# Product-key weights in chunks of 16 by 8 keys, with both log products of a step in row halves of TensorE

## What is computed

```python
q = (x @ Wq_pk).reshape(b, n, P, HEADS, DIM_KEY)              # P = 2, HEADS = 8
sim = einsum('pbnhd,pkhd->pbnhk', q, pk_keys)                 # two sets of 64 keys
scores, idx = top_k(sim, 16)
score = scores[0][..., :, None] + scores[1][..., None, :]     # sums of pairs of keys
final_scores, final_indices = top_k(score, 16)
w = softmax(final_scores)
k = einsum('bnhk,bnhkd->bnhd', w, keys_table[final_indices])  # 4096 rows a head, 64 wide
v = einsum('bnhk,bnhkd->bnhd', w, values_table[final_indices])
out = causal_attention(q2, k, v) @ Wo                         # q2 = x @ Wq
```

## Time and profile before

| | |
|---|---|
| median of 3 runs | 1949.09 us (1947.84 to 1950.35) |
| profiled execution | 1947.92 us |
| its span | 1946.1 us, granted clock 0.99 |
| TensorE busy | 1868.8 us, 96% |
| weight loads | 1400.6 us, 72% |
| DVE busy | 1608.5 us, 83% |
| ACT busy | 1453.3 us, 75% |
| POOL busy | 1317.2 us, 68% |
| DMA engines | 11.5% on SP's queue |

### The profile page before, as it was taken

The page is one execution under the profiler, slowest core; times in us unless marked ns, Lnnn a source line. Parts: engine busy times, 40 slices in busy tenths (PEclk is TensorE's granted clock), DMA queues, the critical chain, the costliest instruction groups (busy, mean ns, idle before and its releaser), DMA issues.

```text
span 1946.1 us, 43717 instructions
## 1 busy us (share of the span) xinstructions
PE 1868.8 (96%) x11464; PEld 1400.6 (72%) x11464; DVE 1608.5 (83%) x4824; ACT 1453.3 (75%) x2969; POOL 1317.2 (68%) x1576
## 2 busy tenths in 40 slices
PE   5997899999999999999999999999999999999997
PEld 3765577777777777777777777777777777777775
DVE  3646788888888888988888888888888888888886
ACT  3763477777877777877777777777877777877775
POOL 1112477777777777777777777777777777777775
PEclk9998999999999999999999999999999999999998
DMA  3001110001000200020000200020001100020001
GB/s 108 2 1 47 57 22 20 20 17 61 18 20 20 65 18 16 18 64 20 20 17 17 61 20 20 20 62 17 17 20 37 48 16 16 18 64 20 20 19 28
DMA packets 118622, 58.00 MB, mean 30 GB/s; under 512 B 110224, under 2 KB 116560, under 8 KB 117261
## 3 DMA queue, kind: packets, MB, share of 16 engines
q1 hardware_dynamic: 115778, 56.75, 11.5%
q10 hardware_dynamic: 2795, 0.70, 0.2%
HBM read 24.55 MB, written 0.70 MB: 13 GB/s over the span
## 4 chain that ended last, share of the span: by engine, by line
PE 70%; issue 10%; POOL 7%; ACT 2%; DVE 1%; POOLq 0%; ACTq 0%; SPq 0%; DMA 0%; DVEq 0%
PE ps L980 24%; PE ps L971 14%; PE ps L988 13%; PE ps L992 7%; POOL k_W_low L1399 4%; PE ps L1074 3%; PE ps L1025 2%; PE ps L1066 2%; PE ps L1029 2%; PE ps L1020 1%; ACT k_W_high L1213 1%; PE ps L1015 1%; PE ps L1002 1%; PE ps L1008 1%; ACT k_qT L1233 1%
## 5 line engine op out<-in xcount | busy, mean ns | idle before, releaser
L1399 POOL TENSOR_TENSOR k_W_low<-k_W,k_W_high 128x688 fp32r<-128x688 f32 x513 | 852.1, 1661 | 360.4 <-ACT k_W_high L1213 360.4
L1208 ACT ACTIVATE k_W<-ps 128x688 f32<-128x688 f32 x1029 | 770.0, 748 | 366.0 <-PE ps L971 355.9
L1565 DVE SCALAR_TENSOR_TENSOR k_W<-ps,k_W 128x688 f32<-128x688 f32 x1028 | 887.2, 866 | 154.9 <-ACT k_W L1208 149.0
L980 PE MATMUL ps<-k_W,k_tab 128*128 128x344 f32 x2048 | 676.7, 453 | 0.0
L971 PE MATMUL ps<-k_X,sel 128*128 128x344 f16 x2058 | 473.2, 312 | 7.6 <-DVE k_W L1565 7.5
L980 PEld LDWEIGHTS ps<-k_W,k_tab 128*128 128x128 f32 x2048 | 366.6, 190 | 127.0 <-issue 0.5
L1213 ACT ACTIVATE k_W_high<-k_W 128x688 fp32r<-128x688 f32 x513 | 397.7, 775 | 0.0
L988 PE MATMUL ps<-k_W_high,k_tab_high 128*128 128x344 f32 x1024 | 386.1, 379 | 0.0
L971 PEld LDWEIGHTS ps<-k_X,sel 128*128 128x128 f16 x2058 | 160.9, 98 | 234.1 <-issue 94.6
L988 PE MATMUL ps<-k_W_high,k_tab_low 128*128 128x344 f32 x1024 | 324.0, 319 | 0.0
L992 PE MATMUL ps<-k_W_low,k_tab_high 128*128 128x344 f32 x1024 | 246.3, 322 | 0.0
(11 more groups left out here) (234 smaller groups left out, 2295.7 us busy)
## 6 DMA issues: line engine op xcount, KB each, us to landing
k_tab<-in_tables SPq DMA_DIRECT2D x9, 2048.0 KB, 7.3
k_X<-k_spl SPq DMA_TRANSPOSE x390, 2.4
k_xs<-x2T SPq DMA_DIRECT2D x66, 86.0 KB, 2.0
k_qT<-k_qs SPq DMA_DIRECT2D x33, 86.0 KB, 2.0
cst<-in_consts SPq DMA_DIRECT2D x1, 1024.0 KB, 20.2
wts<-in_weights SPq DMA_DIRECT2D x1, 896.0 KB, 12.9
cst<-in_consts SPq DMA_DIRECT2D x1, 874.5 KB, 17.5
xr<-in_xrows SPq DMA_DIRECT2D x1, 750.0 KB
```

Of the source, the lines that this page charges most:

```text
L980: mm = mm_(sums, tab[:, slot, at + k, :], W[:, d % RING, k, :], start=(d == 0 and k == 0), stop=(d == NDC - 1 and k == 1))
L1208: A(W[:, d % RING, :, :], ps[:, 2 * (d % 2):2 * (d % 2) + 2, 0:LOUT], ACT.Exp).then_inc(e_done, 1)
L1399: G.tensor_tensor(W_low[:, q % SPLIT_RING, :, :], W[:, d % RING, :, :], W_high[:, q % SPLIT_RING, :, :].bitcast(F32), ALU.subtract).then_i ...
L1565: V.scalar_tensor_tensor(W[:, d % RING, :, :], ps[:, 2 * (d % 2):2 * (d % 2) + 2, 0:LOUT], 0.0, W[:, d % RING, :, :], ALU.is_ge, ALU.mult) ...
```

## The change

- A chunk is now 16 keys of one set by 8 of the other (before 4 by 32). The scores of a chunk need 64 rows of `X` instead of 128, so a step's two log products use rows 0 to 63 and rows 64 to 127. `sel` shrinks from 2 x 8 matrices to 2 and is made from the unit matrix by four sums on POOL.
- `X` has 8 column groups instead of 4, one for two steps. The first two come from three transposes; SP then waits for them and fills the other six with ten copies of 32 partitions within the chip.
- The order of the chunks changes (`WINDOWS`, `chunk_of`), and the table is loaded in that grouping: 16 DMAs of 16 partitions, in runs of 512 B, instead of one DMA with 16 KB a partition. The semaphore counts change with it (`NLOAD`, `NMOVE`).
- `aS` and `spl` go from 480 to 384 elements a partition, and the clamp is one instruction instead of two.
- On ACT `copy_queries` at step 6 moves ahead of `weights_high` and `high_part`.

The number of matmuls, their columns and their order stay as they are.

```diff
-        WINDOW = (0, 2, 3, 1)
+        WINDOWS = (((0, 0), (1, 1)), ((2, 2), (3, 3)), ((0, 1), (1, 0)), ((2, 3), (3, 2)),
+                   ((2, 0), (3, 1)), ((0, 2), (1, 3)), ((2, 1), (3, 0)), ((0, 3), (1, 2)))
+        NMOVE = 160
+        NLOAD = 16 * 18
...
-        X = sb("X", [128, 2, 4, XW], F16)
+        X = sb("X", [128, 2, 8, XW], F16)
...
+        def chunk_of(d, k):
+
+            i, j = WINDOWS[d // 2][k]
+            return 16 * (i % 2) + 8 * (i // 2) + 4 * (j // 2) + 2 * (j % 2) + d % 2
...
-                    sync.dma_start(tab[:, slot, :, :], t).then_inc(s_tab[slot], 16)
+                    for u in range(2):
+                        for v in range(4):
+                            at = 64 * u + 16 * v
+                            for i2 in range(2):
+                                sync.dma_start(tab[at:at + 16, slot, 16 * i2:16 * i2 + 16, :], t[v, i2, :, :, u, :]).then_inc(s_tab[slot], 16)
...
                     wait_alone(sync, low_step, n + 1)
-                    for odd, done in ((0, x_even), (1, x_odd)):
-                        for t, (t0, m) in enumerate(TT):
-                            rows = -(-m // 16) * 16
-                            sync.dma_start_transpose(X[:, par, odd::2, t0:t0 + rows],
-                                                     spl[0:rows, t, odd:odd + 4, :, :].rearrange("p b x j -> p (b x j)")).then_inc(done, 16)
+                    for t, (t0, m) in enumerate(TT):
+                        rows = -(-m // 16) * 16
+                        sync.dma_start_transpose(X[:, par, 0:2, t0:t0 + rows],
+                                                 spl[0:rows, t, :, :, :].rearrange("p b x j -> p (b x j)")).then_inc(x_even, 16)
+                    wait_alone(sync, x_even, n * 48 + 48)
+                    for half in range(2):
+                        first = X[64 * half:64 * half + 32, par, :, :]
+                        second = X[64 * half + 32:64 * half + 64, par, :, :]
+                        other = X[96 - 64 * half:128 - 64 * half, par, :, :]
+                        sync.dma_start(first[:, 2:4, :], first[:, 0:2, :]).then_inc(x_odd, 16)
+                        for w in range(2):
+                            sync.dma_start(first[:, 4 + w::2, :], first[:, 1 - w:2 - w, :].to_broadcast([32, 2, XW])).then_inc(x_odd, 16)
+                        sync.dma_start(second[:, 4:6, :], second[:, 0:2, :]).then_inc(x_odd, 16)
+                        sync.dma_start(second.rearrange("p (s w) t -> p s w t", w=2)[:, 1::2, :, :],
+                                       other[:, None, 0:2, :].to_broadcast([32, 2, 2, XW])).then_inc(x_odd, 16)
...
                 def log_weights(i, par, d):
                     for k in range(2):
-                        c = 2 * d + k
-                        mm = mm_(ps[:, 2 * (d % 2) + k, 0:LOUT], sel[:, (c // 8) % 2, c % 8, :], X[:, par, c // 8, 0:LOUT], start=True, stop=True)
+                        rows = slice(64 * k, 64 * k + 64)
+                        mm = mm_(ps[:, 2 * (d % 2) + k, 0:LOUT], sel[rows, d % 2, :], X[rows, par, d // 2, 0:LOUT], start=True, stop=True)
                     mm.then_inc(log_mm, 1)
...
+                            if d == 6 and par == 0:
+                                copy_queries(g)
                             if (d + LEAD - 2) % NDC in SPLITS:
...
                             if d == 6:
                                 high_part(i + 1)
-                                if par == 0:
-                                    copy_queries(g)
...
                 def clamp_scores(n):
                     wait_alone(pool, a_ready, n * 2 + 2)
-                    G.tensor_scalar(aS[:, :, 4, :], aS[:, :, 0, :], -NEG, FAR, ALU.min, ALU.max).then_inc(clamped, 1)
-                    wait_alone(pool, clamped, n * 2 + 1)
-                    G.tensor_scalar(aS[:, :, 0:4, :], aS[:, :, 0:4, :], -NEG, FAR, ALU.min, ALU.max).then_inc(clamped, 1)
+                    G.tensor_scalar(aS[:, :, :, :], aS[:, :, :, :], -NEG, FAR, ALU.min, ALU.max).then_inc(clamped, 1)
```

More of the change, by code:

```diff
@@ L234, in _ @@
                 pool.wait_ge(s_const, 16)
-                nc.gpsimd.tensor_copy(sel[:, :, :, :].rearrange("p w c m -> p (w c m)"), const("sel")).then_inc(cast_done, 1)
+                eye = const("eye")
+                for half in range(2):
+                    r, q = 64 * half, 64 * half + 32
+                    nc.gpsimd.tensor_tensor(sel[r:r + 32, :, :].rearrange("p c (b a) -> p (c b) a", a=16),
+                                            eye[r:r + 32, None, r:r + 16].to_broadcast([32, 16, 16]),
+                                            eye[r:r + 32, None, r + 16:r + 32].to_broadcast([32, 16, 16]), ALU.add).then_inc(cast_done, 1)
+                    pool.wait_ge(cast_done, 2 * half + 1)
+                    nc.gpsimd.tensor_tensor(sel[q:q + 32, :, :].rearrange("p c (b a) -> p (c b) a", a=16),
+                                            eye[q:q + 32, q:q + 16, None].to_broadcast([32, 16, 16]),
+                                            eye[q:q + 32, q + 16:q + 32, None].to_broadcast([32, 16, 16]), ALU.add).then_inc(cast_done, 1)
+                    pool.wait_ge(cast_done, 2 * half + 2)
                 nc.gpsimd.tensor_copy(eyeb[:, :], const("eye")).then_inc(cast_done, 1)
@@ L788, in part_of @@
             return t[:, slot, bass.ds(pair * (2 * NPART) + half * NPART, NPART), :]
+        def chunk_of(d, k):
+            i, j = WINDOWS[d // 2][k]
+            return 16 * (i % 2) + 8 * (i // 2) + 4 * (j // 2) + 2 * (j % 2) + d % 2
         def rows_of(slot, pair, half):
-            first = FIRST_ROW[half]
+            odd = tab[:, slot, :, :].rearrange("p (n c) d -> p n c d", c=2)
             if isinstance(pair, int):
-                return tab[:, slot, 8 * pair + first:8 * pair + first + NPART, :]
-            return tab[:, slot, bass.ds(pair * 8 + first, NPART), :]
+                at = (2 * pair + half) * NPART
+                return odd[:, at:at + NPART, 1, :]
+            return odd[:, bass.ds(pair * (2 * NPART) + half * NPART, NPART), 1, :]
         def score_area(t, pj):
@@ L976, in table_sum @@
                     if d not in SPLITS:
-                        at = 8 * WINDOW[d // 4] + 2 * (d % 4)
                         pe.wait_ge(w_done, i * NDC + (d + 1))
                         for k in range(2):
-                            mm = mm_(sums, tab[:, slot, at + k, :], W[:, d % RING, k, :], start=(d == 0 and k == 0),
+                            mm = mm_(sums, tab[:, slot, chunk_of(d, k), :], W[:, d % RING, k, :], start=(d == 0 and k == 0),
                                      stop=(d == NDC - 1 and k == 1))
@@ L983, in table_sum @@
                         q = split_at(d)
-                        at = 2 * (WINDOW[d // 4] * len(SPLIT) + SPLIT.index(d % 4))
+                        at = [chunk_of(d, k) // 2 for k in range(2)]
                         pe.wait_ge(high_done, i * NSPLIT + (q + 1))
```

32 lines of the change are left out of this document (15 added, 17 removed).

## The result

| | before | after |
|---|---|---|
| median | 1949.09 us (1947.84 to 1950.35) | 2104.73 us (2101.70 to 2104.76) |
| ratio after : before | | 1.0795 (95%: 1.0776 to 1.0813) |
| span of the profiled execution | 1946.1 us | 2099.8 us |
| items, first product of L1002 / L1033 to the last | 234.5 to 1928.8 | 238.6 to 2083.0 |

The kernel became 155.6 us slower. The forecast was 2070 us with a range of 2035 to 2150: the direction and the main mechanism were right, and the forecast was 35 us too low. Behind these 35 us stand errors of both signs, which the runs take apart.

What follows compares the result with a forecast made beforehand. The prediction took TensorE's streaming of passes, 0.144 us each, to set the pace. It summed 1947.9 + 151 (turns) - 26 (queries' copy) - 3 (DVE waits) = 2070 us, plus 0 to 8 for the table load; range 2035 to 2150.

Steps and rivals of the forecast that it cites:

- the main mechanism: On TensorE, turns between 128 and 64 rows around each step's log products cost more than the 0.144 us pass saved.
- The sign, and why: Slower: each step pays 0.305 us for turns and weights less 0.144 for the pass saved, +0.161 us; chance of slower 0.91.
- The open question on f16 weights of 64 rows: Log products' weights behind the turn in: put at 0.01 us; if as slow as float32 ones, +91 us.
- one-pass float32r weights might need only half: Table products behind the turn out: if float32r weights need only half of 0.105 us, -27 us.
- The turn term, +151 us: Sixteen steps at +0.161 us, less 0.21 at the step behind the attention: +2.37 us an item, times 64 items.
- 151 - 26 - 3: Sum over the run: turns +151 us, queries' copy moved forward -26, small waits on DVE absorbed -3.
- an item of 28.8 us: Sign to look for in the profile after: one head of one sequence takes 28.8 us; before, 26.47 us.
- The copy of the queries, -26: TensorE's 0.82 us wait before the mask product, 32 times, goes whole: -26 us; nothing of this item late next.
- 2 us in hand: Ten copies on SP's queue land at about 787.1, needed at 788.08 plus 1.1 us of later PE: hidden.
- Rival 3: Ten copies land late: from 0.7 us a copy, each further 0.1 costs 64 us; 2130 us at 0.8; chance 0.09.
- The table load, +8: Sixteen pieces, eight times in the run, delay the transposes on SP's queue: +8 us at most; ends 0 and 80.
- Rival 4: The table load blocks the transposes, 4 to 10 us in eight items: 2100 to 2150 us; chance 0.07.

Runs made afterwards that it cites:

- the small product: Kernel before plus an 8-column f16 product of 64 rows ahead of each step's two log products: 2125.49 us; control with 128 rows: 1971.74 us.

## Why the prediction was right, and where it was not

The medians make a ladder: before 1949.1; copy of the queries moved forward 1930.9; with the new chunks and ten copies 1972.6; with row halves 2049.9; with the table in pieces 2104.7. The steps are -19 (against the kernel before in its own job), +42, +77 and +55 us. Not every step of a ladder is a cost by itself: the +42 are waits for the ten copies, and once the row halves come in they are hidden again. Read without them, the row halves and chunks together cost 2049.9 - 1930.9 = 119 us.

- **The sign, and why: right.** In an item without a copy of the queries, 13 of 16 steps grew by 0.15 to 0.17 us, where 0.161 was forecast. Each part stands in the trace after: table product 0.25 behind the log products, so 0.095 for the turn out and 0.01 for the f16 weights; 0.10 more for the float32 products. The open question on f16 weights of 64 rows is settled by the small product: two turns with f16 weights come to 0.18 in an ordinary step, a little under the 0.19 + 0.02 of my terms, so they are not as dear as float32 ones. That one-pass float32r weights might need only half is refuted as well: from the log products to the second record of the table product it is 0.51 after and 0.45 before with one pass of 0.144 more, so turn out and weights together take 0.20 there too, and those steps grew as much as the float32 ones (0.15 both). The Trainium skill, page "TensorEngine Tiling (Array Packing)", section "Key Properties", says that changing the tiling mode drains TensorE; the traces agree, with 0.09 to 0.10 us a turn.
- **The turn term, +151 us: too large.** An item without the copy went from 25.70 to 27.61, +1.91 us, against 2.37 forecast (2.32 with the DVE waits). Laid beside each other step by step, the missing 0.46 is in three places. Thirteen ordinary steps pay 0.155 instead of 0.161 (0.08). The attention's step gave back 0.14, not 0.05 (0.09): behind the attention, the log products overlap with the last products of 64 rows, in the timeline above at 1032.00 while those of 1031.82 run. And two steps, the one ahead of the turned probabilities and the one that holds them, cost 0.03 together and not 0.32: the first had 0.16 of idle time before, which took up its turns (1.62 us against 1.46 for its like; 1.61 now), and in the second the six products of the probabilities take 0.65 to the log products behind them where they took 0.67, so the turn into 64 rows shows no cost at that place. Why it is free there was not tried. Together with the copy of the queries, the items of the kernel with one load are 1.17 and 1.91 us longer than before, 98.6 us in 64, against 122 in the sum (151 - 26 - 3). The prediction's sign "an item of 28.8 us" did come true, (2083.0 - 238.6) / 64, but by luck: the ordinary items take 28.31 and 27.61, and the stalls at the heads make up the rest.
- **The copy of the queries, -26: right in size, wrong in what comes next.** The step lost 0.81 us, but alone the move is worth 19. "Nothing" was to be late next; it was the transposes, 0.26 us further down. In the kernel after, the slower steps cover that, and the items with the copy grew by 0.74 us less than the others (1.17 against 1.91): 24 of the 26.
- **The ten copies, "2 us in hand": right for the wrong reason.** They take 0.59 to 0.61 us each to issue, 0.65 with the gap, where I took 0.56 (SP's queue of the kernel after, one ordinary item):

```profile
657.30 0.61 SPq L878 DMA_DIRECT2D k_X<-k_X  x1
657.95 1.31 SPq L880 DMA_DIRECT2D k_X<-k_X  x2
```

  The slack was not 2 us: in the kernel after the last copy lands 0.72 us (median) before the log products that read it, and in items with a copy of the queries 0.15. From the first issue to the last landing the ten take 8.0 us where I had 7.1. The slack that there is comes from the delay that the turns bring: take the turns out, and an item is 0.37 or 0.96 us longer for the copies. Rival 3 had the mechanism; it needed a faster TensorE, not a slower copy. I had reckoned TensorE's side with only the turns in it, and called the rest spare.
- **The table load, +8: the term that failed.** I priced the issues at 0.37 to 1.27 us each; they take 0.78, 12.46 for sixteen, and are in time. What I named and gave no price were the packets: 2 MB in 512 B runs keep the DMA engines full until 718, at 98 to 103 GB/s, while one piece of 16 KB runs lands in 7.3 us; what is issued behind it lands behind it. Median landing of a piece, 7.7 us, says little, since it is from its own issue. 55 us came of it, within the ends of 0 and 80: the seven long items are 52.4 us over their neighbours. Rival 4 described it, with 4 to 10 us in eight items and 2100 to 2150 us, and got 0.07. It deserved more, since the landing of the transposes behind 4096 packets had no row that bounded it. The Trainium skill, page "DMA: Bandwidth & Descriptors", section "Specifications", names 512 B as the smallest transfer for line rate; here runs of just that size moved at about a third of what 16 KB runs did (2 MB in 7.3 us is 287 GB/s), so the measurement decides.
- **The sum.** All but the table load came to 100 us (2049.9 less 1950.0 in the same job), the table load to 55: 1949.1 + 155 = 2104. The forecast's 122 + 0 was some 22 us too much on one side and 55 too little on the other; the range held the time by the table load's upper end. That the time fell inside the range is in part luck: two errors of opposite sign, of which the larger was in a term taken at 8 us at most.

## What to carry to other kernels

Here two products of 64 rows side by side save one pass, 0.144 us, and a switch in and out between neighbours of 128 rows costs about 0.30 us with float32 weights behind it (0.18 with f16): by these numbers a run of packed products has to save more than two passes, so count the neighbours, not the pair. That longer runs pay is not shown: the one run that halved the turns lost more to waits. Price a transfer by its packets as well as by its issues, for everything that is queued behind it. "Hidden with slack" is a statement about both sides: say how the slack changes when the bound engine speeds up, and after a wait is removed look for the next late thing in the same item.

## What was not expected of the hardware

- **A standstill costs more than its length.** In each of the seven waits for the transposes, 4.15 to 7.44 us long, the granted clock goes to 0.50 before the wait is over, and it comes back only 3 to 6 us after TensorE has started again. At the head shown it is half from 717.2 to 724.0, with TensorE standing until 718.93; behind the longest wait of the kernel after,

```profile
488.59 0.47 PE L1003 MATMUL ps<-k_X,sel 64*128 64x344 f16 x2 [7.44 <-DMA k_X<-k_spl]
```

  it is half from 485.1 to 491.9. The seven waits sum to 37.1 us and the seven items are 52.4 us over their neighbours: 2.2 us each beyond the wait. The kernel before has no such spell between 250 and 1930 us: its granted clock there is 1.00. The Trainium skill, page "TensorE: Matmul & The Clock Gate", section "HAM oscillation — how this bites in real kernels", describes waits on DMA after which TensorE starts at half its rate; these traces agree, in a kernel that is otherwise always busy.
- **The price of a turn depends on what is loaded behind it**: 0.0965 us a step more behind float32 or float32r weights than behind f16 ones, by two kernels that differ only in the place of a product of 8 columns.
- A copy within the chip from 32 rows takes SP 0.60 us to issue, a load of 256 runs 0.78, a load of 128 runs of 16 KB 0.36.
